# Median search of the gates: five steps within ±1.5, a one-pass penalty, fewer steps for z, and the second group's gates at other places

## The reference, cut to what matters

```python
x = x + conv(_ln_c(x))        # conv: x * g, one gate g per batch and channel
#   u   = stack(mean, max, std of each of 512 channels)   -> 1536 values per batch
#   med = median(u)                                       -> mean of the two middle values
#   z   = sum((u - med)**3 * cfc_w) / sqrt(1 + eps) * bn_w + bn_b;  g = sigmoid(z)
t = _to_tokens(x)             # 8 batches x 256 tokens, 512 channels
t = t + ffn(_ln_t(t))         # shared expert on all tokens + the best one of 8 experts per token
```

## Time and profile before

| what | value |
|---|---|
| median of 3 runs | 409.06 us (407.67 to 409.27) |
| the profiled execution itself | 408.12 us |
| its span, first to last instruction | 406.4 us |
| TensorE busy | 384.3 us, 95% |
| VectorE / ScalarE / GpSimd busy | 63% / 40% / 34% |
| mean granted TensorE clock | 0.982 |

### The profile page before, as it was taken

The page is one execution under the profiler, slowest core; times in us unless marked ns, Lnnn a source line. Parts: engine busy times, 40 slices in busy tenths (PEclk is TensorE's granted clock), DMA queues, the critical chain, the costliest instruction groups (busy, mean ns, idle before and its releaser), DMA issues.

```text
span 406.4 us, 6811 instructions
## 1 busy us (share of the span) xinstructions
PE 384.3 (95%) x1976; PEld 305.4 (75%) x1979; DVE 255.8 (63%) x501; ACT 160.8 (40%) x274; POOL 137.3 (34%) x195
## 2 busy tenths in 40 slices
PE   5864999999999999999999999999999999999994
PEld 2421688887876788888888888888888888888883
DVE  6888776746575676869865557456365654676222
ACT  3876546446511124331115353154264415354110
POOL 7689333300000111106040344426425442545201
PEclk9969799999999999999999999999999999999999
DMA  8900040011110722342340578636646772752300
GB/s 309 413 8 0 26 156 27 26 53 52 53 52 27 284 79 78 99 151 96 123 131 26 185 242 325 233 84 252 220 156 234 290 254 88 267 182 74 93 31 30
DMA packets 14764, 55.96 MB, mean 138 GB/s; under 512 B 2575, under 2 KB 2575, under 8 KB 11280
## 3 DMA queue, kind: packets, MB, share of 16 engines
q1 hardware_dynamic: 9936, 40.93, 28.1%
q0 software_dynamic: 4800, 14.69, 10.1%
HBM read 43.02 MB, written 13.63 MB: 139 GB/s over the span
## 4 chain that ended last, share of the span: by engine, by line
PE 86%; DVE 5%; ACT 4%; POOL 2%; issue 2%; DMA 1%; DVEq 0%; POOLq 0%; ACTq 0%
PE GU L1516 47%; PE yb L1516 23%; PE th L1508 4%; PE tx L1501 4%; PE th L1545 2%; DVE search_junk L903 1%; ACT x_sb L593 1%; DMA x_sb<-x_tok 1%; PE mb L1516 1%; ACT scratch L611 1%; PE mb L1494 1%; ACT scratch L607 1%; PE th L1373 1%; PE yb L1553 0%; ACT w_parts L626 0%
## 5 line engine op out<-in xcount | busy, mean ns | idle before, releaser
L1516 PE MATMUL GU<-w_parts,xT 128*128 (+1 forms) x864 | 214.5, 396 | 0.2 <-DVE xT L1080 0.2
L1516 PEld LDWEIGHTS GU<-w_parts,xT 128*128 128x128 f32 x864 | 158.0, 188 | 31.5 <-DVE xT L1080 0.4
L1516 PE MATMUL yb<-w_parts,hT 128*128 (+1 forms) x420 | 102.8, 393 | 0.0
L1516 PEld LDWEIGHTS yb<-w_parts,hT 128*128 128x128 f32 x420 | 77.8, 188 | 15.6
L660 ACT ACTIVATE hT<-th 128x512 fp32r<-128x512 f32 x36 | 21.5, 597 | 159.5 <-PE th L1508 159.5
L533 POOL DMA_INDIRECT out<-x_sb,scatidx x20 | 37.3, 1866 | 92.7 <-DVE x_sb L1306 83.5
L1071 DVE TENSOR_TENSOR w_parts<-w_raw,w_parts 128x2048 f32 (+1 forms) x24 | 54.9, 2288 | 7.4 <-issue 7.2
L583 ACT ACTIVATE w_parts<-w_raw 128x2048 f32 (+1 forms) x24 | 45.2, 1911 | 4.1 <-issue 4.0
L1055 DVE TENSOR_TENSOR hidden<-hidden,GU 128x512 f32<-128x512 f32 x36 | 24.7, 687 | 34.4 <-PE GU L1516 34.3
L1049 DVE TENSOR_TENSOR hT<-th,hT 128x512 fp32r<-128x512 f32 x36 | 24.8, 689 | 28.0 <-ACT hT L660 27.7
L496 POOL TENSOR_TENSOR x_rstd<-x_mv,eps 128x1 f32<-128x1 f32 x16 | 3.0, 190 | 99.9 <-DVE x_mv L1019 99.9
(11 more groups left out here) (278 smaller groups left out, 349.6 us busy)
## 6 DMA issues: line engine op xcount, KB each, us to landing
w_raw<-weights SPq DMA_DIRECT2D x27, 1024.0 KB, 5.3
x_sb<-x_tok SPq DMA_DIRECT2D x8, 512.0 KB, 7.7
xn_d<-tiles SPq DMA_DIRECT2D x16, 256.0 KB, 2.0
z_d<-x_sb SPq DMA_DIRECT2D x16, 256.0 KB, 2.0
tiles<-xn_d,tokidx POOLq DMA_INDIRECT x20, 4.6
x_sb<-z_d,tokidx POOLq DMA_INDIRECT x20, 5.5
out<-x_sb,scatidx POOLq DMA_INDIRECT x20, 6.8
conv<-conv_par SPq DMA_DIRECT2D x1, 10.0 KB, 6.3
```

The lines of the kernel that those rows point to most:

```text
L1516: last = pe.matmul(dst, left[:, lp, kc, :], wset(q, k, wp, kc), start=(i == 0), stop=(i == 3 * KC - 1))
```

## The change

The number of rounds goes from 6 to 5 and the interval from ±24 to ±1.5. The penalty for the second value is made from the values in one instruction, and the counting for `middle` comes behind `least_here`. z is formed with the factors in another order, with -bn_b as a fourth term of the sum that is written once ahead of the search. `keep_warm` counts around the tail change, and the order of the two TensorE steps there. In the second group each step of the tail stands earlier in the queues, and n = 6 has the same order as its neighbours.

```diff
...
 RING = 4
-SEARCH_FROM, SEARCH_TO = -24.0, 24.0
-SEARCH_STEPS = 6
+SEARCH_FROM, SEARCH_TO = -1.5, 1.5
+SEARCH_STEPS = 5
...
 PREPARED = ((), (3,), (4,), (5,), (6,), (7,), (8,), (9, 10), (11, 12), (13, 14), (15,))
-LATE = 6
+SECOND_SET_IN = 6
...
         stats = stats_f.rearrange("p b (k s) -> p b k s", s=3)
-        stats_tmp = search_junk[:, 2 * P:2 * P + GROUP * KC * 3].rearrange("p (b s) -> p b s", b=GROUP)
+        z_terms = sb("z_terms", [P, GROUP, KC, 4])
+        cubes = search_junk[:, 2 * P:2 * P + GROUP * KC * 3].rearrange("p (b k s) -> p b k s", b=GROUP, k=KC)
...
                     load_w(1, DOWN)
-                if n == LATE:
+                if n == SECOND_SET_IN:
...
                     scan_second(2)
-                if n == LATE:
+                if n == 5:
...
                     scan_second(3)
-                if n == 4:
-                    scan_second(5)
...
             own(dve.tensor_scalar(cw_ks, cw_ks, -1.0 / (1.0 + BN_EPS) ** 0.5, None, ALU.mult))
+            bnb = conv[:, 4 * KC:5 * KC].unsqueeze(1).to_broadcast([P, GROUP, KC])
+            own(dve.tensor_scalar(z_terms[:, :, :, 3], bnb, -1.0, None, ALU.mult))
...
-            def count_upto_v1(values, space, g):
-
-                dve.tensor_scalar(space[:, 0, :], values, v1, 0.0, ALU.is_le, ALU.add, accum_out=counts_bf[:, 1:2]).then_inc(v1_counted, 1)
-                dve.wait_ge(v1_counted, g + 1)
-                own(dve.tensor_scalar(space[:, 0, :], space[:, 0, :], BIG, None, ALU.mult))
+            def least_above_v1(values, space):
+
+                own(dve.tensor_scalar(space[:, 0, :], values, v1, BIG, ALU.is_le, ALU.mult))
                 least_here(values, space, search[:, 10:11])
+                dve.tensor_scalar(space[:, 2, :], values, v1, 0.0, ALU.is_le, ALU.add, accum_out=counts_bf[:, 1:2]).then_inc(v1_counted, 1)
...
             least_of_batch(tx[:, 0:P], slice_junk, v1)
-            count_upto_v1(slices, slice_junk, 0)
+            least_above_v1(slices, slice_junk)
...
-                rows, here = stats_f[:, group(g), :], z[:, group(g), :]
-                cw = conv[:, 0:KC * 3].unsqueeze(1).to_broadcast([P, GROUP, KC * 3])
-                medians = spread.rearrange("p (b r) -> p b r", b=GROUP)[:, :, 0:1]
+                rows, here, terms = stats[:, group(g), :, :], z[:, group(g), :], z_terms[:, :, :, 0:3]
+                cw = cw_ks.unsqueeze(1).to_broadcast([P, GROUP, KC, 3])
+                medians = spread.rearrange("p (b r) -> p b r", b=GROUP)[:, :, 0:1].unsqueeze(3)
                 dve.wait_ge(medians_ready, g + 1)
-                own(dve.tensor_tensor(stats_tmp[:, :, :], rows, medians.to_broadcast([P, GROUP, KC * 3]), ALU.subtract))
-                own(dve.tensor_tensor(rows, stats_tmp[:, :, :], stats_tmp[:, :, :], ALU.mult))
-                own(dve.tensor_tensor(rows, rows, stats_tmp[:, :, :], ALU.mult))
-                own(dve.tensor_tensor(stats_tmp[:, :, :], rows, cw, ALU.mult))
-                own(dve.tensor_reduce(here, stats_tmp[:, :, :].rearrange("p b (k s) -> p b k s", s=3), AX_X, ALU.add))
-                bnb = conv[:, 4 * KC:5 * KC].unsqueeze(1).to_broadcast([P, GROUP, KC])
-                dve.tensor_tensor(here, here, bnb, ALU.subtract).then_inc(z_ready, 1)
+                own(dve.tensor_tensor(cubes, rows, medians.to_broadcast([P, GROUP, KC, 3]), ALU.subtract))
+                note(dve.tensor_tensor(rows, cubes, cubes, ALU.mult))
+                own(dve.tensor_tensor(cubes, cubes, cw, ALU.mult))
+                own(dve.tensor_tensor(terms, rows, cubes, ALU.mult))
+                dve.tensor_reduce(here, z_terms[:, :, :, :], AX_X, ALU.add).then_inc(z_ready, 1)
...
                     count_second(0)
-                if n == 5:
-                    count_second(5)
-                for t in first if n != LATE else ():
+                for t in first:
...
                 if n == 5:
-                    raise_second(5)
-                    own(dve.tensor_scalar(junk_second[:, 0, :], slices_second, low, BIG, ALU.is_lt, ALU.mult))
-                    least_here(slices_second, junk_second, search[:, 9:10])
-                if n == LATE:
-                    gate_inputs(1, spread_second(2))
+                    dve.wait_ge(least_spread, 4)
+                    dve.wait_ge(n_upto_v1, 2)
+                    least_of_batch(spread_second(1), junk_second, m2)
+                    middle(tally_second(SEARCH_STEPS))
...
                     x_lo(t, t % RING)
-                for t in first if n != LATE else ():
+                for t in first:
...
                 if n == 5:
-                    dve.wait_ge(least_spread, 3)
-                    least_of_batch(spread_second(0), junk_second, v1)
-                    count_upto_v1(slices_second, junk_second, 1)
-                for t in first if n == LATE else ():
-                    gate_tile(t, t % RING, t // 2)
+                    gate_inputs(1, spread_second(2))
...
                     raise_second(4)
+                    own(dve.tensor_scalar(junk_second[:, 0, :], slices_second, low, BIG, ALU.is_lt, ALU.mult))
+                    least_here(slices_second, junk_second, search[:, 9:10])
                 for t in first:
-                    if n == LATE:
-                        norm_tile(t, t % RING)
...
                     raise_second(2)
-                if n == 5:
-                    dve.wait_ge(least_spread, 4)
-                    least_of_batch(spread_second(1), junk_second, m2)
-                    dve.wait_ge(n_upto_v1, 2)
-                    middle(tally_second(SEARCH_STEPS))
+                if n == 4:
+                    dve.wait_ge(least_spread, 3)
+                    least_of_batch(spread_second(0), junk_second, v1)
+                    least_above_v1(slices_second, junk_second)
...
             to_all(tx[:, 0:P], 9).then_inc(least_spread, 1)
-            keep_warm(2)
+            keep_warm(3)
+            pe.wait_ge(least_ready, 2)
+            to_all(tx[:, P:2 * P], 10).then_inc(least_spread, 1)
...
             pe.matmul(tally(SEARCH_STEPS), mates, counts_bf[:, 1:2], start=True, stop=True).then_inc(n_upto_v1, 1)
-            pe.wait_ge(least_ready, 2)
-            to_all(tx[:, P:2 * P], 10).then_inc(least_spread, 1)
+            keep_warm(2)
...
             to_all(tx[:, 2 * P:3 * P], 7).then_inc(medians_ready, 1)
-            keep_warm(5)
+            keep_warm(6)
...
                 if n == 5:
-                    tally_below(5)
-                if n == LATE:
-                    spread_medians()
+                    spread_least(1)
+                    tally_v1()
...
                 if n == 5:
-                    spread_least(0)
+                    spread_medians()
...
                     tally_below(1)
-                if n == LATE:
-                    spread_gate(4)
...
                 if n == 5:
-                    tally_v1()
-                    spread_least(1)
+                    spread_gate(4)
...
                     tally_below(2)
-                if n == LATE:
-                    prepare(8)
+                if n == 4:
+                    spread_least(0)
...
                 up_product(n + 1, (n + 1) % RING, (n + 1) % 2, 0, 0, lambda: amid_up(n))
-                for t in first if n != LATE else ():
+                for t in first:
```

More of the change, by code:

```diff
@@ L126, in program @@
         counts_bf = sb("counts_bf", [P, 2], BF16)
-        slice_junk = hidden[:, 1, 0:2 * P].rearrange("p (a c) -> p a c", a=2)
+        slice_junk = hidden[:, 1, 0:3 * P].rearrange("p (a c) -> p a c", a=3)
         raw_gate = w_raw[:, GATE, :, :].rearrange("p k c -> p (k c)")
@@ L131, in program @@
         slices_second = raw_up[:, NV:NV + P]
-        junk_second = raw_up[:, NV + P:NV + 3 * P].rearrange("p (a c) -> p a c", a=2)
+        junk_second = raw_up[:, NV + P:NV + 4 * P].rearrange("p (a c) -> p a c", a=3)
         warm = sb("warm", [P, 2])
```

## The result

The changed kernel takes 403.94 us (median of 4 runs, 403.83 to 404.03) against 409.09 us (407.67 to 409.27, 4 runs): ratio 0.9892, interval 0.9871 to 0.9913. Its profiled execution took 403.9 us with a span of 402.1, where the one before had 408.12 us: 4.2 us less, and the sum had 4.1. The medians lie 5.15 us apart, because the profiled execution of the kernel before was 0.97 shorter than its median; where its longer executions lose that time no trace shows.

A forecast was written before the change was run, and what follows sets the result against it. TensorE was taken to bound the kernel (86% of the last chain), paying where it waits: start and shared expert. 408.12 - 2.6 - 1.5 = 404.0, plus 0.4 towards the runs' average, gave 404.4 us, range 402.3 to 406.4.

The forecast's parts named there:

- the term from the profiled execution to the runs: Whole kernel: 0.4 us added because the profiled execution was below the average of it and the three runs, 408.53.
- The median's spread: Start: with one round fewer and the shorter second penalty, the spread starts at 37.8 instead of 40.76.
- The count behind `least_here`: Start: the count just fits into the return trip of the least, cost 0 to 0.1 us, taken as 0.
- z held by GpSimd: Start: z's two-SBUF-operand products wait for GpSimd's L489, so gates start +1.3 us later (0 to 1.4); chance 0.50.
- The sum of the start: Search to first product: -2.6 us in all (-2.1 held at half clock; not held -3.9).
- The terms -1.85 and -1.1: Start: one search round fewer, -1.85 us; second penalty made by one comparison, -1.1 us.
- The step from the gates to the first mix: Start: the first mix begins 1.45 us after the gates, at 42.05.
- The second group: Shared expert, n = 4 to 6: 31.29 us against 32.83, so -1.5; -0.3 if each slack is missed by 0.4.
- The slacks of 0.2, 0.3 and 0.3: Second group: margins by which first least, median and gates are ready before TensorE reaches them, in us.
- GpSimd does not hold z: Rival, start: z's products run unheld, the start gives 3.9 us, time 403.1; chance 0.27.
- the late and the exposed tail: Rivals, second group: waits become TensorE's, 405.7, chance 0.13; TensorE stands through the whole tail, 409.3 to 409.4, chance 0.03.
- The half clock falls on products: Rival, start: half clock covers the first products, costing 3.2 us, time 407.6; chance 0.07.

The follow-up runs named there:

- the operand in PSUM: Changed kernel with z's difference also written to PSUM, so each product of z reads one operand from SBUF and one from PSUM: 402.65 us.
- six rounds: Changed kernel with the first group alone searching six rounds between -24 and 24 again, the second group keeping five: 404.53 us.
- z free: Changed kernel with z's difference also in PSUM and six rounds in the first group: 404.75 us, 2.10 above the free z with five rounds.
- the late tail: Changed kernel, five rounds kept, but the second group's tail and gates at their old places in n = 5 and 6: 405.73 us.
- four rounds: Changed kernel with the first group alone searching four rounds between -1.5 and 1.5: 404.18 us.

## Why the prediction was right

**The verdict and the time.** 403.94 lies in the range of 402.3 to 406.4 and 0.46 below 404.4. Of this 0.4 is the term from the profiled execution to the runs: the change's profile (403.9) agrees with its median. The reason is partly shown: with the old `keep_warm`s the changed kernel's runs spread over 1.08 us, with the new ones over 0.20. That the spread of before has the same source was not tried on it, and its mean granted clock alone does not explain it: beside the first four runs it took 407.43 us at 0.990, but 408.96 and 409.15 at 0.991. The two other errors, 0.2 too much at the start and 0.3 too little in the second group, cancel, and that is luck.

**The median's spread.** Forecast at 37.8, found at 37.87. The count behind `least_here` costs nothing: L927 starts at 36.76, 0.72 after L923's 36.04, the return time of the earlier trace rows.

**z held by GpSimd.** The mechanism is shown by the operand in PSUM (1.29 us) and by six rounds (0.21 for the same square with GpSimd idle). The term was mis-sized: free z takes 1.10 and not 1.0, and the hold 2.57 - 1.10 = 1.47 and not 1.3, just beyond its bound of 1.4. The sentence that failed is "the square waits until 38.8, and the last product until 40.04": the square let the end of a GpSimd instruction at 38.87 (25.34 + 11 x 1.23) pass and waited for the next one too, and then nothing was left to hold the rest. The prediction's evidence was weaker than it took it to be: L932 reads one operand, and so was no sample of products that read two; L516, held beside L1071, was the nearer row. The rule cited from the Trainium skill, page "SBUF — State Buffer", section "Who interferes with whom", agrees with the changed kernel and these two runs as to which instruction is held: 1.69 us with two operands in SBUF, 0.20 with one, 0.21 with GpSimd idle. That the square stood through a second instruction goes beyond it. The row that spoke against it, L1199 beside L515, stays as it was, and was not tried.

**The sum of the start.** The terms -1.85 and -1.1 were added as if each stood alone, and the hold set against them. The sum came out (2.40 against 2.6), but single terms are not worth their length: undone alone, the round costs 0.59 (0.44 up to the first product) and the pass 0.04, since the end of L490 sets the end or the free start of z either way. The second penalty's 1.06 us of the earlier trace rows was not its length: the same pass, at another place beside GpSimd, took 0.45. With z free a round is worth 2.10 (2.01 up to the first product). The step from the gates to the first mix was forecast at 1.45 and took 1.48.

**The second group.** -1.84 against -1.5. The slacks of 0.2, 0.3 and 0.3 were 0.25, 0.55 and 0.23, so no wait reached TensorE, and n = 4 came out at 10.29 against 10.28. Two terms were too large: n = 5 took 10.74 and not 10.88, and n = 6 took 9.96 and not 10.13. That the places and not the round pay is shown by the late tail (1.79).

**The rivals.** "GpSimd does not hold z" falls with the operand in PSUM; the late and the exposed tail fall with the three slacks. "The half clock falls on products" did not come about, and the run with the old counts says why: it is the longer `keep_warm`s that keep it away, and without them it reaches the gates' products, not the long ones, and costs 0.62 us in the median and not 3.2. The half clock of the kernel before lay from 39.8 to 46.6 by the granted 0.95 and 0.84 of the earlier trace rows, a little longer than the 39.9 to 46.3 of this rival.

## What to carry to other kernels

A step taken out of a chain pays only down to the point where the next link is held by another engine; look for what that engine is doing at the earlier time before adding up lengths. Where VectorE multiplies small tiles with both operands in SBUF beside a long run of GpSimd, try one operand in PSUM, which here cost one instruction of 0.2 us and gave back 1.3. When a chain gets shorter, look at the granted clock of the stretch too, since the idle time ahead of the products has changed with it.

## What was not expected

A chain of instructions with two SBUF operands does not slip in together where one GpSimd instruction ends and the next begins: with four rounds three products in a row each stood for one instruction (1.13, 1.30, 1.19 us), though each needs 0.2. Nor does a held instruction always come in at the next such boundary. The square issued at 38.47 in the changed kernel let one pass 0.4 us later (38.87), and the one issued at 38.51 with the old `keep_warm`s (1.53 us) let one pass 0.24 later (39.98 - 1.23 = 38.75). The three products with four rounds, which had waited 1 us and more, came in at the first. L934 with its one operand, issued at 36.10 and so some 0.4 ahead of a boundary (25.40 + 9 x 1.23 = 36.5), came in there. What decides this is open and was not tried.
